# Attention scores in column tiles: issuing each 128-partition score product as four products of 32 output partitions

## The reference, cut to what matters

```python
def _L0_attn_ref(x, w_qkv, w_out, b_out):
    ...
    scale = 1.0 / jnp.sqrt(jnp.array(Hd, dtype=x.dtype))
    logits = jnp.einsum('bhqd,bhkd->bhqk', q, k) * scale
    mask = jnp.tril(jnp.ones((T, T), dtype=x.dtype))
    big_neg = jnp.array(-10000000000.0, dtype=x.dtype)
    logits = logits + (1.0 - mask)[None, None, :, :] * big_neg
    attn = jax.nn.softmax(logits, axis=-1)
    out = jnp.einsum('bhqk,bhkd->bhqd', attn, v)
    ...
```

## Time and profile before

| | |
|---|---|
| median of 3 runs | 4613.62 us (4610.97 to 4613.92) |
| span of the profiled execution | 4604.9 us |
| attention, first maxima to last output | about 799 to 1760 us of the span |
| PE busy over the whole span | 87% |
| DVE, POOL, ACT busy over the whole span | 66%, 51%, 51% |

### The profile page before, as it was taken

The page is one execution under the profiler, slowest core; times in us unless marked ns, Lnnn a source line. Parts: engine busy times, 40 slices in busy tenths (PEclk is TensorE's granted clock), DMA queues, the critical chain, the costliest instruction groups (busy, mean ns, idle before and its releaser), DMA issues. The chain is left out here.

```text
span 4604.9 us, 118970 instructions
## 1 busy us (share of the span) xinstructions
PE 4004.3 (87%) x49612; PEld 2550.1 (55%) x49612; DVE 3057.2 (66%) x5400; ACT 2329.4 (51%) x3872; POOL 2369.6 (51%) x1536
## 2 busy tenths in 40 slices
PE   4499798999999997559979799699999999997799
PEld 3366554233333334336647444387778778876577
DVE  6411154888888885631137477599899899997575
ACT  2122133577777772011226378667777776774233
POOL 1145444222222224124523265399999999998454
PEclk7699899899999998679989999899999999999899
DMA  7323366656555636332332466633333433332662
GB/s 211 113 47 51 78 215 218 94 94 94 94 94 93 94 60 219 94 105 48 55 72 74 145 246 244 212 90 100 96 96 95 101 104 91 96 101 80 253 225 81
DMA packets 339597, 549.38 MB, mean 119 GB/s; under 512 B 55488, under 2 KB 239200, under 8 KB 339040
## 3 DMA queue, kind: packets, MB, share of 16 engines
q1 hardware_dynamic: 285552, 467.46, 38.7%
q0 software_dynamic: 24576, 34.10, 4.6%
q10 hardware_dynamic: 28912, 40.02, 2.4%
HBM read 335.69 MB, written 212.32 MB: 119 GB/s over the span
## 5 line engine op out<-in xcount | busy, mean ns | idle before, releaser
L2539 POOL TENSOR_TENSOR s_hc<-s_hs,s_ct 128x1024 f32<-128x1024 f32 x512 | 1213.3, 2385 | 66.8 <-DVE s_hs L2518 52.0
L2518 DVE TENSOR_TENSOR_SCAN s_hs<-s_dA,s_psB 128x1024 f32<-128x1024 f32 x512 | 1168.3, 2286 | 100.0 <-POOL s_hc L2539 30.0
L2442 PE MATMUL s_psB<-s_diag,s_duT 128*32 128x128 f32 x32768 | 962.9, 275 | 75.8 <-DVE s_hs L2518 51.0
L2442 PEld LDWEIGHTS s_psB<-s_diag,s_duT 128*32 128x32 f32 x32768 | 910.1, 111 | 180.6 <-issue 94.0
L1389 DVE CUSTOM_DVE_ANT_0 a_masked<-a_psM,k_later 128x1024 f32<-128x1024 f32 (+7 forms) x1024 | 724.9, 750 | 146.0 <-PE a_psM L1447 142.7
L1371 ACT ACTIVATE a_wt<-a_psE 128x512 f32<-128x512 f32 (+1 forms) x1216 | 625.3, 579 | 267.5 <-PE a_psE L1473 257.8
L2383 ACT ACTIVATE s_dA<-s_dlt,s_aneg 128x1024 f32<-128x1024 f32 x512 | 587.9, 1148 | 341.4 <-DVE s_hs L2518 336.8
L1350 POOL TENSOR_SCALAR_AFFINE_SELECT a_wt<-a_wt 128x512 f32<-128x512 f32 x256 | 162.4, 634 | 692.3 <-ACT a_wt L1371 692.3
L2363 ACT ACTIVATE s_diag<-s_ident,s_bt 128x128 f32<-128x128 f32 x956 | 317.6, 388 | 13.4 <-ACT s_ys L2372 13.4
L1447 PE MATMUL a_psM<-a_kst,a_qst 96*128 96x512 bf16 (+3 forms) x1152 | 306.6, 331 | 14.7 <-DVE a_mx L1389 10.8
L1473 PE MATMUL a_psE<-a_qst,a_kst 99*128 99x512 bf16 (+3 forms) x1152 | 309.1, 330 | 6.7 <-ACT a_wt L1371 6.5
(11 more groups left out here) (366 smaller groups left out, 6242.4 us busy)
## 6 DMA issues: line engine op xcount, KB each, us to landing
s_dlt<-dd SPq DMA_DIRECT2D x128, 512.0 KB
a_qst<-qs SPq DMA_DIRECT2D x144, 128.0 KB
a_kst<-ks SPq DMA_DIRECT2D x144, 128.0 KB
yd<-s_ys ACTq DMA_DIRECT2D x33, 512.0 KB
vs<-a_va ACTq DMA_DIRECT2D x32, 512.0 KB, 3.6
zsd<-s_zs SPq DMA_DIRECT2D x32, 512.0 KB, 2.7
ucd<-s_uc SPq DMA_DIRECT2D x8, 2048.0 KB, 9.3
dd<-s_dl SPq DMA_DIRECT2D x32, 512.0 KB, 4.2
```

Source lines behind the costliest of these rows:

```text
L2442: ins = pe.matmul(psB[s][DG * m:DG * (m + 1), c * P:(c + 1) * P], duT[j % 2][:, c, DG * r:DG * (r + 1)], diag[:, place(NB * g + m, u), c, ...
L2518: dve.tensor_tensor_scan(hs[k % 2][:, :], dA[k % 2][:, :], psB[s][:, :], 0.0, ALU.mult, ALU.add).then_inc(scanned, 1)
L2539: pool.tensor_tensor(hc[NB * (g % 2) + r][:, :], hs[k % 2][:, :], ct[:, g, :], ALU.mult).then_inc(weighed, 1)
```

## The change

Three products are cut along their output partitions into pieces of `QC` = 32: the score product, the product for the maxima, and the turning of the maxima (96 output partitions, so three pieces). Each piece has 32 weight columns and the same moving data as the whole had, and writes its 32 partitions of the same bank. The semaphore is raised by the last piece alone. Nothing else changes, and no instruction changes its place.

```diff
+QC = AUG
...
                     for c in range(0, (j + 1) * P, BANK):
                         r = min(BANK, (j + 1) * P - c)
-                        ins = pe.matmul(psM[:, place[u] + c:place[u] + c + r], qst[g % HG][0:SK, x, j * P:(j + 1) * P],
-                                        kst[g % HG][0:SK, x, c:c + r], start=True, stop=True)
+                        for m in range(0, P, QC):
+                            ins = pe.matmul(psM[m:m + QC, place[u] + c:place[u] + c + r],
+                                            qst[g % HG][0:SK, x, j * P + m:j * P + m + QC],
+                                            kst[g % HG][0:SK, x, c:c + r], start=True, stop=True)
                     ins.then_inc(m_ready, 1)
...
-                    pe.matmul(psM[0:PARTS * GH * LT, place[u]:place[u] + P], mp[:, :, :].rearrange("p k n -> p (k n)"),
-                              identb[:, :], start=True, stop=True).then_inc(m_ready, 1)
+                    for m in range(0, PARTS * GH * LT, QC):
+                        ins = pe.matmul(psM[m:m + QC, place[u]:place[u] + P],
+                                        mp[:, :, :].rearrange("p k n -> p (k n)")[:, m:m + QC],
+                                        identb[:, :], start=True, stop=True)
+                    ins.then_inc(m_ready, 1)
...
                     for x in range(c):
-                        ins = pe.matmul(psE[s % NE][:, x * (q1 - q0):(x + 1) * (q1 - q0)],
-                                        kst[g % HG][0:SK + PARTS, x0 + x, kt * P:(kt + 1) * P],
-                                        qst[g % HG][0:SK + PARTS, x0 + x, q0:q1], start=True, stop=True)
+                        for m in range(0, P, QC):
+                            ins = pe.matmul(psE[s % NE][m:m + QC, x * (q1 - q0):(x + 1) * (q1 - q0)],
+                                            kst[g % HG][0:SK + PARTS, x0 + x, kt * P + m:kt * P + m + QC],
+                                            qst[g % HG][0:SK + PARTS, x0 + x, q0:q1], start=True, stop=True)
                     ins.then_inc(e_ready, 1)
```

## The result

The changed kernel takes 4585.06 us (median of four runs, 4584.4 to 4598.9), the kernel before 4613.77: a ratio of 0.9944, 95% interval 0.9929 to 0.9959. The forecast was 4561 us, 53 less; 29 less came (26 by the ratio). The direction is right and the time lies in the range, but the forecast gain is about twice the measured one, so its sum was wrong. One run of the kernel before (11483 us) and one of a kernel of the experiments (5458 us, three lots with the lighter maximum) fell into a slower state of the chip and are left out of every comparison.

The account below looks back on a forecast made before the run. PE was taken to bound the attention, save a DVE-bound stretch in each group, losing time to tile-shape changes. 57 + 1 - 4 - 1 = 53 us less, from 4613.6 to 4561 us; range 4530 to 4604.

Parts of the forecast that it names:

- The stops belong to the tile shape: PE around attention's value units: changing between 128 and 32 weight columns causes stops; 0.22 us a unit removed, load included.
- half rate: Rival, attention's score and maxima products: four bf16 streams do not fit side by side; 4930 us, chance 0.10.
- a stop that stays: Rival, attention's value units: bf16 against fp32 alone also causes the stop; 4618 us, chance 0.07.
- loads that no longer hide: Rival, 128-column rounds in attention: four weight loads one after the other take 0.12 us; 4592 us, chance 0.13.
- More and smaller products: Attention on PE: 12288 products for 3072 add late last pieces and unhidden first loads where PE restarts; 4 us.
- What reaches the end: Attention groups: 0.3 us gained in DVE's stretch, 1.54 in seven other units; 1.84 a group, 57 us in 31.
- the forecast 1: Attention's tail, with no maxima left: some 1 us gained of the last group's 2.6, ACT being close behind.
- another wait takes the place: Rival, attention: DVE's stretch grows or the maxima's DMA delays, so only four units a group gain; 4586 us, chance 0.17.
- The maxima's DMA: Turning to the next group's first score: three groups already wait for this DMA and keep their time; 1.3 us.
- the bounds given for the forecast: Cost 0 to 15 us, DVE's stretch 0 to 0.5 us a group, DMA 1 to 8 us; 4547 to 4583 us.

Follow-up runs that it names:

- three lots with the lighter maximum: Changed kernel with its 13 loads issued in three lots and DVE taking the maximum over at most 256 columns: 4644.07 us, ratio 1.0067.
- the turning put back: Changed kernel with the turning of the maxima as one product of 96 output partitions again: 4595.09 us, ratio 0.9964.
- the lots moved: Changed kernel with loads in three lots, the middle one (four loads) ahead of the output stores: 4558.0 us, ratio 0.9888.
- three lots: Changed kernel with its 13 loads issued in three lots, the middle one right before the maxima's DMAs, full maximum: 4662.78 us, ratio 1.0115.

## Why the prediction was wrong

- **The stops belong to the tile shape, 0.22 us a unit: right**, by the timeline after and by the turning put back. Of the rivals, half rate, a stop that stays and loads that no longer hide are all out: rounds of 512 and 128 columns (0.22 and 0.055 us) keep their pace.
- **"More and smaller products", 4 us: the step that failed.** I priced the pieces as work of the array, with bounds of 0 and 15 us, and not as instructions that must be fetched. The late fetches cost some 16 us of idle time, and behind four of the stops PE ran 20 us at half clock, in which it does half the work: some 26 us by this count. With the loads spread out the kernel takes 4558 us for 4585; in ratios, 0.0056 or 26 us. That is what was missing: 4558 to 4565 us is about what the sum had forecast (4561).
- **What reaches the end, 57 us: somewhat too much.** With the lots moved a group takes (1673.7 - 822.5) / 31 = 27.46 us, 1.42 less than before, where the sum had 1.84 less the costs, 1.66: 44 us in 31 groups for 51. Counted by the distance between starts (waits of over 0.15 us), PE's waits for DVE rise from 52 to 82 us between 860 and 1690 us, 30 for the 25 that the sum gave to DVE, and those for ACT, which it put at nothing outside the tail, from 10 to 17. Head and tail of the attention give some 4 us for the forecast 1, and the last 4 of the 52 us between the medians are not in the two traces, so they are scatter. That 4558 comes so near to 4561 is in part luck.
- **The rival "another wait takes the place" gave 4586 us, and 4585 came: luck.** Its mechanism, a longer wait for DVE or for the maxima's DMA, is not what cost the 26 us: these came back when the loads were moved, while PE's waits for DVE stayed as long (80 us with the change, 82 with the lots moved, counted in the same way).
- **The maxima's DMA, 1 us: too small, harmless here.** PE's weight loads wait 0.7 us for it before and 7.4 after. That it has so little room was seen; that loads could take the room was not, and three lots showed it at 59 us.
- **Two numbers on the way.** The prediction put 8.7 us between the profiled span and the timed median. In every run on record a timed execution is 1.7 to 1.8 us longer than its span, so the other 7 us were scatter: the profiled execution before lay below the median, and its span is only 21.7 us above that of after where the medians are 29 apart. The 53 us do not rest on this. And the bounds given for the forecast, added up, make 4550 to 4588 us, not 4547 to 4583.

## What to carry to other kernels

Cutting products into more instructions changes what an engine must fetch: count blocks of 256 instructions, see how long one lasts, and look whether bursts of loads fill the DMA engines for longer. A stop in the middle of one product, with "issue" behind it, is the mark of a late fetch; the cure here was to spread the loads, and the place of each lot decided, since a lot just ahead of a small urgent DMA cost more than the fetch did. Where tile shapes alternated on PE, each change cost about 0.10 us whatever the type, and using the narrower shape throughout removed it.

## What the hardware showed that was not expected

Instruction fetches wait behind ordinary loads: at the median of all packets from 840 to 1700 us a 16 KB packet starts 213 PE records ahead of the place in the block where the stops stand, and 248 in the kernel before; in the ten late cases it started 0 to 100 ahead. Of the ten stops, those of 1.5, 1.8, 2.4 and 2.6 us were followed by 6.8, 3.4, 3.4 and 6.8 us at a granted clock of 0.50 (1.2 GHz); one of 1.9 us was not. A round of four bf16 column tiles with 128 columns takes 0.055 us, as one whole product of 128 weight columns does.
